# Attention units of one head by two key tiles by half of the queries, three PSUM banks for the side jobs, and projection rounds five units apart

## What is computed

```python
x = x + attention(layernorm_over_channels(x))        # 8 heads of 24, q and k l2-normalised
t = tokens(x)
t = t + mixture(layernorm_over_tokens(t))            # 4 experts of 192 -> 768 -> 192, the best 2 of 4
# attention, per image:
q, k, v = qkv(x);  q, k = l2norm(q), l2norm(k)
out = softmax(q @ k.T * temperature) @ v;  out = out @ proj_w.T + proj_b
```

## Time and profile before

| what | us |
| --- | --- |
| median of 3 runs | 2734.44 |
| lowest and highest | 2732.74, 2734.46 |
| the profiled execution | 2724.55 |
| its span, first to last instruction | 2722.8 |
| prologue, up to the first scores | 101.09 |
| attention phase, first scores to the end of its matmuls | about 1540 |

### The profile page before, as it was taken

The page is one execution under the profiler, slowest core; times in us unless marked ns, Lnnn a source line. Parts: engine busy times, 40 slices in busy tenths (PEclk is TensorE's granted clock), DMA queues, the critical chain, the costliest instruction groups (busy, mean ns, idle before and its releaser), DMA issues. The chain is left out here.

```text
span 2722.8 us, 58859 instructions
## 1 busy us (share of the span) xinstructions
PE 2467.2 (91%) x18693; PEld 1299.5 (48%) x18693; DVE 1672.2 (61%) x4869; ACT 1780.4 (65%) x2228; POOL 1422.4 (52%) x1137
## 2 busy tenths in 40 slices
PE   4699999999989989999999974999999999999975
PEld 3333333333333333333333322777777777777755
DVE  5556766766766776686676655555555555555522
ACT  2587777777778777777777852555555555555542
POOL 3334435534543543554454333677777777777750
PEclk8799999999999999999999986999999999999987
DMA  4121112112112111211211353444444444444419
GB/s 100 51 59 36 49 48 59 48 43 62 49 48 51 54 43 49 59 48 42 54 50 52 79 175 135 154 159 171 158 160 171 157 160 173 155 160 174 154 73 340
DMA packets 160582, 276.56 MB, mean 102 GB/s; under 512 B 21828, under 2 KB 129844, under 8 KB 150884
## 3 DMA queue, kind: packets, MB, share of 16 engines
q1 hardware_dynamic: 141908, 245.43, 27.9%
q0 software_dynamic: 13392, 27.97, 2.8%
q10 hardware_dynamic: 5056, 0.42, 0.2%
HBM read 174.07 MB, written 49.69 MB: 82 GB/s over the span
## 5 line engine op out<-in xcount | busy, mean ns | idle before, releaser
L802 ACT ACTIVATE probs<-ps_s 128x1024 f32<-128x1024 f32 x1024 | 1012.1, 1023 | 282.5 <-PE ps_s L701 275.0
L1374 POOL TENSOR_TENSOR h_split<-h_f,h_split 128x512 f16<-128x512 f32 x444 | 552.0, 1244 | 237.2 <-ACT h_f L1351 230.0
L1347 ACT ACTIVATE h_split<-ps_h,packs 128x512 f16<-128x512 f32 x444 | 305.2, 687 | 391.2 <-PE ps_h L1301 391.0
L1301 PE MATMUL ps_h<-m_xn_t,packs 128*128 128x512 f16 x2220 | 553.6, 380 | 0.5 <-DVE m_xn_t L1436 0.5
L714 PE MATMUL ps_o<-probs,v_aug 128*32 128x512 f32 x4096 | 549.4, 609 | 0.4 <-ACT probs L802 0.4
L1068 POOL TENSOR_TENSOR inv_norm<-sumsq,minus_half 128x16 f32<-128x16 f32 x128 | 378.0, 2953 | 305.7 <-DVE sumsq L1011 305.7
L1315 PE MATMUL ps_y<-packs,h_split 128*128 128x192 f16 x5328 | 511.9, 245 | 0.6 <-POOL h_split L1374 0.6
L1315 PEld LDWEIGHTS ps_y<-packs,h_split 128*128 128x128 f16 x5328 | 453.1, 97 | 105.1 <-POOL h_split L1374 1.1
L701 PE MATMUL ps_s<-stacks_odd 98*128 98x512 f16 x1024 | 300.9, 385 | 16.6 <-DMA stacks_odd<-heads 9.9
L701 PE MATMUL ps_s<-even 98*128 98x512 f16 x1024 | 299.5, 383 | 11.3 <-ACT probs L802 5.7
L1351 ACT ACTIVATE h_f<-ps_h,packs 128x512 f32<-128x512 f32 x444 | 302.0, 680 | 0.0
(11 more groups left out here) (213 smaller groups left out, 2805.2 us busy)
## 6 DMA issues: line engine op xcount, KB each, us to landing
packs<-expert_pack SPq DMA_DIRECT2D x74, 1635.0 KB, 6.9
even<-heads SPq DMA_DIRECT2D x192, 96.0 KB, 2.3
stacks_odd<-heads SPq DMA_DIRECT2D x192, 96.0 KB, 2.4
tile_rows<-sorted_rows SPq DMA_DIRECT2D x37, 400.0 KB, 6.6
tokens<-in_x_dram SPq DMA_DIRECT2D x17, 768.0 KB, 5.4
y_in<-y_tokens SPq DMA_DIRECT2D x16, 768.0 KB, 8.7
out_dram<-y_out SPq DMA_DIRECT2D x16, 768.0 KB, 6.7
even<-heads SPq DMA_DIRECT2D x128, 48.0 KB
```

Of the source, the lines that this page charges most:

```text
L802: act.activation(probs[:, u % PRING, :], ps_s[:, u % 2, :, :].rearrange("p f n -> p (f n)"), ACT.Exp).then_inc(s_probs, 1)
L1301: mm = pe.matmul(ps_h[:, n % HBUF, :], w1(par, slot, w, k), xn_t[0:rows_k, par, c, :], start=(i == 0), stop=(i == 4))
L1347: act.activation(h_split[:, n % HSPLIT, 0, :], ps_h[:, n % HBUF, :], ACT.Gelu, bias=bias1(par, slot, k), scale=1.0 / WSCALE)
L1374: pool.tensor_tensor(h_split[:, n % HSPLIT, 1, :], h_f32[:, n % HBUF, :], h_split[:, n % HSPLIT, 0, :], ALU.subtract).then_inc(s_h, 1)
```

## The change

1. A unit is now one head by **two key tiles** by **half of the queries**. An image has four phases of 16 units (`PHASE`), each one group of 4 heads and one half of the queries. The two score matmuls of a unit have different key tiles and the same queries.
2. `ps_o` has **one bank**. A phase accumulates its 8 `pv` calls there, and VectorE takes it at unit 4 of the following phase (`TAKE_AT = 4`). The first `pv` of a phase waits for that.
3. The `pv` calls stay at the odd units, but the first of a phase goes from the unit 5 to unit 6 of the phase (`PV_UNITS`).
4. `ps_m` has **three banks** (`BANKS`). Job n waits for job n - 3.
5. `ROUNDS` are five units apart, and no longer four and five in turn. The last `q` moves from unit 56 to unit 60.
6. At unit 0 `scores` waits for the first half of the queries and the first two key tiles only; the other key tiles are waited for at units 4, 8 and 12, the second half of the queries at unit 16.

```diff
-PV_LAG = GH + 1
-PV_AT = range(1, UNITS, 2)
-TAKE_AT = (2, 4)
+PHASE = UNITS // 4
+PV_UNITS = [GH * p + at for p in range(UNITS // GH) for at in ((6, 7) if p % (PHASE // GH) == 0 else (5, 7))]
+TAKE_AT = 4
+BANKS = 3
...
-ROUNDS = tuple(14 + (9 * r + 1) // 2 for r in range(NT + 2))
+ROUNDS = tuple(14 + 5 * r for r in range(NT + 2))
...
-    ps_o = ctx.enter_context(nc.psum_tensor("ps_o", [P, 2, HALF], F32))
-    ps_m = ctx.enter_context(nc.psum_tensor("ps_m", [P, 2, HALF], F32))
+    ps_o = ctx.enter_context(nc.psum_tensor("ps_o", [P, HALF], F32))
+    ps_m = ctx.enter_context(nc.psum_tensor("ps_m", [P, BANKS, HALF], F32))
...
+    def bank_of(img, par, n):
+        return n % 6 if isinstance(img, int) and img == B else (n + par) % BANKS
+
+    def wait_bank(pe, img, par, n):
+
+        if n >= BANKS:
+            wait_taken(pe, img, n - BANKS)
+        elif not (isinstance(img, int) and img == -1):
+            of_bank = [i for i in range(len(jobs_of(img - 1))) if bank_of(img - 1, 1 - par, i) == bank_of(img, par, n)]
+            wait_taken(pe, img - 1, of_bank[-1])
...
     def scores(pe, img, par, u):
-        g, m, j = u // (UNITS // 2), u % (UNITS // 2) // GH, u % GH
+        g, f, pair, j = u // (2 * PHASE), u // PHASE % 2, u % PHASE // GH, u % GH
         h = g * GH + j
         if u == 0:
             pe.wait_ge(s_ones, 2 + 2 * 16)
             for r in range(2):
+                pe.wait_ge(s_rep_q[r], 2 * REP_Q * img + REP_Q)
+        if u == PHASE:
+            for r in range(2):
                 pe.wait_ge(s_rep_q[r], 2 * REP_Q * (img + 1))
-                pe.wait_ge(s_rep_k[r], 2 * REP_K * (img + 1) - REP_K * r)
-        if g == 0 and m == NT - 2 and j == 0:
-            pe.wait_ge(s_rep_k[1], 2 * REP_K * (img + 1))
+        if u < PHASE and j == 0:
+            pe.wait_ge(s_rep_k[pair % 2], 2 * REP_K * img + REP_K * (pair // 2 + 1))
...
-        for f in range(2):
-            mm = pe.matmul(ps_s[:, u % 2, f, :], stacks[par][:, 1, h, m * P:(m + 1) * P],
+        for i in range(2):
+            m = 2 * pair + i
+            mm = pe.matmul(ps_s[:, u % 2, i, :], stacks[par][:, 1, h, m * P:(m + 1) * P],
                            stacks[par][:, 0, h, f * HALF:(f + 1) * HALF], start=True, stop=True)
...
     def pv(pe, img, par, k):
-        p, f = k // 2, k % 2
-        g, m = p // NT, p % NT
+        p, i = k // 2, k % 2
+        g, m = p // NT, p % (PHASE // GH) * 2 + i
-        if m == 0 and not (isinstance(img, int) and img == 0 and g == 0):
-            pe.wait_ge(s_o, 4 * img + 2 * g + f - 1)
+        if m == 0 and not (isinstance(img, int) and img == 0 and p == 0):
+            pe.wait_ge(s_o, 4 * img + p // (PHASE // GH))
...
-            if u in TAKE_AT and has_post(img):
-                take_o(dve, img - 1, 1 - par, 1, TAKE_AT.index(u))
-            if u - UNITS // 2 in TAKE_AT and attend:
-                take_o(dve, img, par, 0, TAKE_AT.index(u - UNITS // 2))
+            if u == TAKE_AT and has_post(img):
+                take_o(dve, img - 1, 1 - par, 1, 1)
+            elif u % PHASE == TAKE_AT and u > TAKE_AT and attend:
+                phase = u // PHASE - 1
+                take_o(dve, img, par, phase // 2, phase % 2)
```

More of the change, by code:

```diff
@@ L545, in _ @@
             for k in range(2):
-                mm = pe.matmul(ps_o[:, 0, 0:NE], ones[0:HC, :], bias_gx[:, k, :], start=(k == 0), stop=(k == 1))
+                mm = pe.matmul(ps_o[:, 0:NE], ones[0:HC, :], bias_gx[:, k, :], start=(k == 0), stop=(k == 1))
             mm.then_inc(s_wg, 1)
@@ L594, in _ @@
             dve.wait_ge(s_wg, 5)
-            st.now(dve.tensor_copy(const_gx[:, :], ps_o[:, 0, 0:NE]))
+            st.now(dve.tensor_copy(const_gx[:, :], ps_o[:, 0:NE]))
             dve.wait_ge(s_wt_free, n)
@@ L641, in job_bank @@
     def job_bank(img, par, n):
-        odd = (jobs_before(img) if isinstance(img, int) else jobs_before(3) + (1 - par) * len(jobs_of(3))) % 2
         if isinstance(img, int) and img == B and n % 6 >= 2:
             return ps_s[:, (n % 6 - 2) // 2, n % 2, :]
-        return ps_m[:, (odd + n) % 2, :]
+        return ps_m[:, bank_of(img, par, n), :]
+    def bank_of(img, par, n):
[6 more added lines that the diff above has]
+            wait_taken(pe, img - 1, of_bank[-1])
     def place_heads(sp, nxt, pair):
@@ L705, in pv @@
     def pv(pe, img, par, k):
-        p, f = k // 2, k % 2
-        g, m = p // NT, p % NT
-        if f == 0:
+        p, i = k // 2, k % 2
+        g, m = p // NT, p % (PHASE // GH) * 2 + i
+        if i == 0:
             pe.wait_ge(s_probs, UNITS * img + GH * p + GH)
-        if m == 0 and not (isinstance(img, int) and img == 0 and g == 0):
-            pe.wait_ge(s_o, 4 * img + 2 * g + f - 1)
+        if m == 0 and not (isinstance(img, int) and img == 0 and p == 0):
+            pe.wait_ge(s_o, 4 * img + p // (PHASE // GH))
         for j in range(GH):
-            mm = pe.matmul(ps_o[32 * j:32 * j + 32, f, :], v_aug[:, par, m, g * GH + j, :],
-                           probs[:, (GH * p + j) % PRING, f * HALF:(f + 1) * HALF], start=(m == 0), stop=(m == NT - 1))
+            mm = pe.matmul(ps_o[32 * j:32 * j + 32, :], v_aug[:, par, m, g * GH + j, :],
+                           probs[:, (GH * p + j) % PRING, i * HALF:(i + 1) * HALF], start=(m == 0), stop=(m == NT - 1))
         mm.then_inc(s_pv, 1)
@@ L731, in pe_job @@
                 wait_taken(pe, img, n - 6)
-        elif not (isinstance(img, int) and img == -1 and n < 2):
-            wait_taken(pe, img, n - 2)
+        else:
+            wait_bank(pe, img, par, n)
         tile = slice(t * P, (t + 1) * P)
@@ L786, in pe_image @@
                 scores(pe, img, par, u)
[L787 to L790, removed]
+            if u in PV_UNITS and attend:
+                pv(pe, img, par, PV_UNITS.index(u))
+            elif u + UNITS in PV_UNITS and has_post(img):
+                pv(pe, img - 1, 1 - par, PV_UNITS.index(u + UNITS))
             for job in jobs_at(img, u):
@@ L825, in take_o @@
     def take_o(dve, img, par, g, f):
-        dve.wait_ge(s_pv, PVS * img + PVS // 2 * (g + 1) - 1 + f)
-        dve.tensor_copy(o_sb[:, par, g, f * HALF:(f + 1) * HALF], ps_o[:, f, :]).then_inc(s_o, 1)
+        dve.wait_ge(s_pv, PVS * img + PVS // 4 * (2 * g + f + 1))
+        dve.tensor_copy(o_sb[:, par, g, f * HALF:(f + 1) * HALF], ps_o[:, :]).then_inc(s_o, 1)
     def dve_job(dve, img, par, n, job, pre, post, route):
```

## The result

The changed kernel takes **2719.79 us** (median of 4 runs, 2715.26 to 2723.2) where the kernel before takes 2733.59 beside it: a ratio of 0.9949, 95% interval 0.9931 to 0.9966. That is faster by 13.8 us, 0.5%. I had forecast 45 us less; the measured time lies inside the range and at under a third of the gain.

What follows compares the result with a forecast made beforehand. PE paces the attention phase, so only its idle time can be regained: 7.3 - 4.3 = 3.0 us per image, times 14 is 42, plus 5.4, minus 2, is 45 less, from 2734.44 to 2689; range 2654 to 2726.

Steps and rivals of the forecast that it cites:

- Start of image 0: First scores of image 0 no longer wait for the last queries' DMA: 5.4 us less, once, bounds 2.7 to 5.4.
- The third bank: Jobs waiting for job n - 2 to leave `ps_m` cost 7.3 us per image; two such waits, 0.5 and 0.55, survive.
- Rival 3: Waits for job n - 2 return as waits for n - 3: only 5 to 20 us less, 2722; chance 0.18.
- Scores and `pv` at nothing: Score matmul and `pv` counts stay, and no longer sharing a key tile costs nothing; bound 100 us.
- three scores in a row: At units 36 to 38 and before unit 54, the third scores wait for the first's exponential: 0.8 and 0.45 us.
- The take: DVE's take of `ps_o` makes each phase's first `pv` wait: 1.4 us at unit 22, 0.6 at unit 6.
- the walk: Stepping through units 22, 6, 38 and 54 with the rows' durations: 3.25 us of new waits per image.
- Exponentials: Scores waiting for an exponential: the earlier 4.0 us in eight images stays, plus 0.8 and 0.45 at units 38 and 54.
- Rounds five apart: Wider rounds in mid-image move work to where nothing waits, as DVE has 30 us per image left; costed at nothing.
- the ten late DMAs: DMAs of the last `q` end in the next image but are wanted only at units 12 and 16, so covered.
- Image 15: Images 0 and 15 lose few bank waits and get new score waits: 2 us more for both.
- The loop's stop: The 2.4 us at every second image's first scores is the hardware loop's turn, not the queries' DMA, and stays.

Runs made afterwards that it cites:

- run 11: Changed kernel with two job banks, the take at unit 3 and rounds four and a half units apart: 2764.6 us, ratio 1.0111 to the kernel before.
- run 6: Changed kernel with the take at unit 3 and rounds four and a half units apart: 2675.91 us, ratio 0.977 to the kernel before.
- run 1: Changed kernel with only the rounds put back to four and a half units apart: 2700.1 us, ratio 0.9857 to the kernel before.
- run 2: Changed kernel with two banks for the jobs where it had three: 2783.02 us, ratio 1.0165 to the kernel before.
- run 4: Changed kernel with the take one unit earlier, at unit 3 of a phase: 2705.45 us, ratio 0.9886 to the kernel before.
- run 8: Kernel before with only the rounds changed, to five units apart: 2772.04 us, ratio 1.0137 to the kernel before.
- run 9: Changed kernel, take at unit 3, rounds 14, 19, 23, 28, 32, then five apart: 2670.97 us, ratio 0.9763 to the kernel before.
- run 10: Changed kernel, take at unit 3, rounds 14, 19, 24, 29, 34, then 38, 42, 47, 51, 56: 2694.01 us, ratio 0.9847 to the kernel before.
- run 5: Changed kernel with the take at unit 3 and `pv` at units 5 and 7 of every pair of units: 2690.51 us, ratio 0.9829 to the kernel before.
- run 7: Changed kernel, take at unit 3, rounds four and a half apart, `pv` at units 5 and 7 of every pair: 2678.55 us, ratio 0.9784 to the kernel before.
- run 12: The kernel of run 10 with `b` of tile 2 moved from unit 32 to 33: 2696.27 us, ratio 0.9854 to the kernel before.

## Why the prediction came out at a third of its gain

**Start of image 0.** Right in kind: no wait is left at the first scores. 3.6 us instead of 5.4, inside the bounds. The start of image 0 scatters from trace to trace: in the thirteen traces with the new units, none of which has a wait there, it lies from 94.8 to 99.5, in the two with the old units at 101.1 and 100.7.

**The third bank.** Right, and about of the right size. I had 7.3 us per image for the two-bank rule, 102 us over 14 images. With take and rounds out of the way the bank is worth 93 us and 6.5 us per image (run 11 against run 6); at the rounds and the take of the change it is 59. The rule of the Trainium skill (Perfetto Trace Analysis, Matmuls), that independent groups should rotate through different PSUM banks, holds here at 59 to 93 us. Rival 3, that the waits only move, is out, although its time (5 to 20 us less, 2722) is nearer to the measured one than mine: the waits for a job bank are gone, and with take 3 and old rounds no others took their place (exponentials 8.6 us in eight images with two banks, 8.5 with three).

**Scores and `pv` at nothing.** Right for the matmuls: 385 and 384 ns in run 6 against 385 and 383. But the units are not free in another way that I did not cost. With two banks, take 3 and old rounds, they are 29 to 30 us slower than the kernel before, 99.04 us per clean image against 96.11, and PE's waits for job banks are some 54 us in eight images where they were 42.3. The three scores in a row cost 0.54 at unit 54 in the change and in runs 1, 2, 4 and 6, whatever the rounds. What else in the order makes the bank waits longer was not taken apart; with three banks they are gone.

**The take.** Right in place and nearly in size: 1.34 at unit 22 where the walk gave 1.4, 0.24 at unit 6 where it gave 0.6, 1.5 us per image in all. Taking it away gave 24 us with the old rounds (run 1 to run 6), more than 14 x 1.5 = 21. The rest fits the half clock beside it: four falls there in the trace of the change, six in that of run 1 (where an image with such a fall alone took 2.3 us longer than a clean one), none in runs 4 and 6. With the wide rounds it gave only 17 (run 4), less than 21: there a clean image got 1.1 shorter and not 1.5, with longer waits at unit 34. The kernel before has stops as long inside its images and no fall beside any of them, so nothing in its rows had pointed there.

**Exponentials.** Here is the missing cost, as the profile shows it. I wrote that only the three scores in a row would wait, 0.8 and 0.45, on top of the 0.5 of before. At those two places it is 0.4 and 0.5 on the mean of the eight images; but all waits for exponentials together are 3.4 us per image, and the rest stands at units that the walk did not look at, 1.1 at unit 34 in seven of the eight images and 0.3 each at 19, 28 and 29. With two banks at the same rounds these waits are 8.9 us in eight images (run 2), with three they are 24.4: while the two-bank rule stopped PE ten times per image, it also kept PE behind ACT. With three banks, take 3 and the old rounds they are 8.5, so they are no price of the bank alone: it takes the wide rounds and the late take to bring them out.

**Rounds five apart: the step that failed.** I wrote that "a wider round moves work to where nothing waits" and costed it at nothing, because DVE has 30 us per image left. The measured price is 25 us with the change (run 1), 30 with take 3 (run 4 to run 6), and 36 on the kernel before (run 8), of which 17 are waits that only the old unit 0 has. So 25 of the 31 us between my forecast and the result are this one term. Without it my forecast image, 93.3, is nearly met by run 1 (93.2), in part by luck: there the takes cost 1.45 us per image where I had 2.0, and the exponentials 2.3 where I had 1.75. Of the price, 18 to 23 us lie in the early half (runs 9 and 10) and none in the late half. The row that goes with it is the wait of the scores of unit 34, 1.4 us per image in run 4 and none in run 6, where a clean image is 1.3 longer. Free time of DVE over a whole image says nothing about this: in the two windows that end at unit 42 DVE is busy for 25 of 29 to 31 us. That the ten late DMAs are covered by the changed unit 0 was right: the even images of run 8, without it, wait up to 1.5 us for queries, and those of the changed kernel do not.

**Image 15.** I took 2 us for images 0 and 15 together; image 15 alone is 7.7 longer. Its last take, at unit 52, comes behind more of DVE's work in the order of jobs that this image has. Here is one stop of 2.2 and half clock beside it:
```profile
1620.15 1.94 PE L730 MATMUL ps_o<-probs,v_aug 128*32 128x512 f32 x8 [2.23 <-DVE o_sb L844]
```
The same stretch is 105.1 in run 1 (old rounds), 104.4 in run 4 (take 3), and 102.2 and 101.7 in runs 6 and 9, so the rounds and the take share in it. How the 7.7 splits beyond that was not taken apart.

**The loop's stop.** It stays, as I had read it. In the runs with old rounds the trace puts the same 2.4 us down to "issue" and no longer to the queries' DMA (9.7 us in 4 times in run 6), which speaks against that DMA. But where the last round is at unit 59 the five stops are longer, 2.7 to 2.9 on the mean (the change and runs 2, 4, 5 and 8) where before and all other runs have 2.1 to 2.5. Whether the late DMA has a part in that was not tested.

**What stays open.** Why a round of five units costs in the early half even when `a` and `b` are moved. The rows show one place: ACT's copy of `n` of tile 4 starts some 1.6 us after the transposes that it waits for are shown as done, and ACT stands idle until then. It does so in 5 to 12 images of every kernel that has three banks and is wide up to unit 34, and in no image of runs 6, 7, 9 and 11. (In run 11 the copy is later still, mostly 2.0 us, but there ACT is busy until it starts. In run 1 ACT stands idle in this way before another copy of `n`, behind a fall of the clock.) But the late copy is not the whole of it. Run 5 has it in 12 images and is 15 us faster than run 4, which has it in 5; and image 9 of run 10, where the copy is only 0.9 late, has the same wait at unit 34 and is as long as image 8, 94.0 us without the loop's stop. There ACT stands idle once more before the exponential behind the copy, for scores that are shown as done at 984.12:
```profile
984.54 0.49 ACT L829 ACTIVATE xn_t<-ps_m 128x384 f16<-128x384 f16 x1 [0.81 <-PE ps_m L784]
...
986.12 2.85 ACT L818 ACTIVATE probs<-ps_s 128x1024 f32<-128x1024 f32 x3 [1.09 <-PE ps_s L717]
```
In both images DVE, too, takes the `b` of that place 1.9 us after its transposes are shown as done. Two engines that see PE late at once point at PE's work there rather than at ACT; that is a reading, since the ends of matmuls are modelled in the trace. No row says what holds it, and no run here removed it alone.

## What to carry to other kernels

A bank, a spacing and an order of takes can each be worth more than the sum of the change: here 93 us gained by the bank and 29, 30 and 17 lost by the units, the rounds and the take were bound up in one edit worth 14. Try each alone, and read the cost of a spacing from the stretch where jobs of both kinds meet, not from the busy share of an image. A stop of PE of 1.3 us or more can cost more than its own length, by the half clock beside it; where one is added, look at the granted clock behind it. The version with the lowest median, three banks, the take at unit 3, and rounds at 14, 19, 23, 28, 32 and from there five apart, takes 2670.97 us, 2.4% under the kernel before; run 6, with the old rounds, is not told apart from it.

## What the runs showed of the hardware that I had not expected

A single stop of PE of 1.31 to 1.34 us, with PE busy on both sides of it, was enough to find the granted clock at half beside it: four times in 12 such stops in the trace of the change, six times in 12 in run 1. The `pv` group behind it took 1.94 instead of 1.07 us. In the traces of all fifteen kernels every fall in images 1 to 14 stood within 2 us of a stop of 1 us or more. The reverse does not hold: the trace of before has 14 stops of 1.3 us or more inside its images (behind DVE's takes of the products) and not one fall beside them, and the 24 stops of 1.31 to 1.51 at unit 34 in runs 4, 10 and 12 have none either. What tells the stops apart that bring a fall, the rows don't show.
